# Two more PSUM evacuations per batch on ScalarE in the late light batches of a routed attention block

## The reference

```
mod = silu(c) @ wmod                      # six rows of 128 per batch: sa, ca, ga, sb, cb, gb
h = layernorm(x) * (1 + ca) + sa
x = x + ga * causal_attention(h)          # one head of 128, "attention"
h = layernorm(x) * (1 + cb) + sb
light  = local_attention(rmsnorm(h))      # 8 heads of 64, windows of 128 rows, then @ wo_light
scores = coordinate_descent(h . token)    # 50 iterations per batch and token, then top_k (128 of 256)
heavy  = attention(rows of h picked by the q scores, all rows weighted by the kv scores)
x = x + gb * (light + scatter(heavy))
```

## Time and profile before

| what | value |
|---|---|
| median of 3 runs | 482.2 us (480.55 to 482.89) |
| profiled execution, its own time | 482.58 us |
| its span | 480.7 us |
| PE busy | 445.8 us (93%) |
| DVE busy | 328.1 us (68%) |
| ACT busy | 345.6 us (72%) |
| POOL busy | 267.3 us (56%) |
| mean granted PE clock | 0.986 |

### The profile page before, as it was taken

One profiled execution on the slowest core, in us unless ns is written; L12 is line 12 of the kernel. 1 busy time (PEld: TensorE's weight loads), 2 busy tenths in 40 slices (PEclk: granted clock), 3 DMA queues, 4 the chain that ended last, 5 costly groups with the idle time before them and its releaser, 6 DMA issues.

```text
span 480.7 us, 12054 instructions
## 1 busy us (share of the span) xinstructions
PE 445.8 (93%) x4088; PEld 393.3 (82%) x4088; DVE 328.1 (68%) x1099; ACT 345.6 (72%) x1260; POOL 267.3 (56%) x325
## 2 busy tenths in 40 slices
PE   7858889999999999899997799999999999999994
PEld 6747688998989988787786688888888888888873
DVE  5874788778768897989879964555555454555551
ACT  3665989889788877677775678667776766677761
POOL 3147576576576776332332335544666666556555
PEclk9996999999999999999999999999999999999998
DMA  6880000001001001000000000100000010000002
GB/s 219 237 314 22 14 13 13 13 1 33 25 1 35 23 20 49 3 12 13 12 12 13 6 8 24 35 18 7 12 11 13 12 18 14 16 12 13 7 8 22
DMA packets 20108, 16.28 MB, mean 34 GB/s; under 512 B 1968, under 2 KB 18880, under 8 KB 19792
## 3 DMA queue, kind: packets, MB, share of 16 engines
q1 hardware_dynamic: 16480, 13.01, 8.8%
q0 software_dynamic: 2816, 2.10, 3.3%
q10 hardware_dynamic: 752, 0.40, 0.3%
HBM read 10.23 MB, written 5.28 MB: 32 GB/s over the span
## 4 chain that ended last, share of the span: by engine, by line
PE 64%; DVE 14%; ACT 5%; issue 4%; POOL 4%; POOLq 0%; ACTq 0%; DVEq 0%
PE bank L905 6%; PE bank L916 6%; PE bank L660 6%; PE bank L931 6%; PE bank L662 5%; PE bank L661 5%; PE bank L813 4%; PE bank L854 4%; PE bank L843 4%; PE bank L827 4%; ACT pr L591 3%; PE bank L872 3%; DVE cd_min L1208 3%; PE bank L944 3%; DVE nmx L1162 2%
## 5 line engine op out<-in xcount | busy, mean ns | idle before, releaser
L420 POOL TENSOR_TENSOR pr<-pr,rinv 128x512 f32<-128x512 f32 x64 | 66.5, 1040 | 84.2 <-DVE rinv L1168 84.2
L432 POOL TENSOR_TENSOR pr<-pr,rinv 128x512 f32<-128x512 f32 x64 | 72.7, 1155 | 63.8 <-DVE rinv L1313 63.8
L591 ACT ACTIVATE pr<-bank,nmx 128x128 f32<-128x128 f32 x256 | 90.5, 377 | 20.8 <-DVE nmx L1162 20.7
L634 ACT ACTIVATE pr<-bank,nmx 128x256 f32<-128x256 f32 x128 | 59.3, 485 | 19.3 <-DVE nmx L1307 19.3
L1307 DVE TENSOR_REDUCE nmx<-bank 128x2 f32<-128x512 f32 x64 | 41.9, 681 | 33.4 <-PE bank L905 33.4
L644 ACT ACTIVATE pt<-bank 128x512 f32<-128x512 f32 x64 | 38.2, 596 | 27.0 <-PE bank L916 27.0
L591 ACT ACTIVATION_READ_ACCUMULATOR pr<-bank,nmx 128x1 f32 x256 | 55.5, 217 | 0.0
L1162 DVE TENSOR_REDUCE nmx<-bank 128x4 f32<-128x512 f32 x64 | 42.8, 672 | 8.5 <-PE bank L813 8.4
L827 PE MATMUL bank<-ident,pr 128*128 128x128 f32 x256 | 38.9, 275 | 7.4 <-POOL pr L420 6.8
L916 PE MATMUL bank<-ident,pr 128*128 128x128 f32 x256 | 38.8, 274 | 1.6 <-ACT pt L644 1.6
L827 PEld LDWEIGHTS bank<-ident,pr 128*128 128x128 f32 x256 | 29.6, 141 | 10.6 <-POOL pr L420 8.5
(11 more groups left out here) (218 smaller groups left out, 1315.8 us busy)
## 6 DMA issues: line engine op xcount, KB each, us to landing
mod_bc<-mod_rows_scratch SPq DMA_DIRECT2D x1, 2560.0 KB, 15.4
X<-in_L_attn_x SPq DMA_DIRECT2D x4, 512.0 KB, 8.0
xh_scratch<-xhs SPq DMA_DIRECT2D x16, 128.0 KB, 1.9
out<-X SPq DMA_DIRECT2D x16, 128.0 KB, 1.8
mod_bc<-mod_rows_scratch SPq DMA_DIRECT2D x1, 1024.0 KB, 7.8
wkv_raw<-in_L_ffn_wkv_light SPq DMA_DIRECT2D x1, 512.0 KB, 7.6
mod_bc<-mod_rows_scratch SPq DMA_DIRECT2D x1, 512.0 KB, 3.8
wmod_sb<-in_L_wmod ACTq DMA_DIRECT2D x1, 384.0 KB, 5.3
```

The lines of the kernel that those rows point to most:

```text
L420: pool.tensor_tensor(q, q, rinv[u][:, :, None].broadcast_to([P, 4, P]), ALU.mult)\
L432: pool.tensor_tensor(q, q, rinv[u][:, 0:2, None].broadcast_to([P, 2, N]), ALU.mult)\
L591: act.activation(pr[u][:, i * P:(i + 1) * P], ps[bank][:, i * P:(i + 1) * P], ACT.Exp, bias=nmx[u][:, i:i + 1], accum_out=sums[u][:, i:i + ...
L634: act.activation(pr[u][:, i * N:(i + 1) * N], ps[bank][:, i * N:(i + 1) * N], ACT.Exp, bias=nmx[u][:, i:i + 1], accum_out=sums[u][:, i:i + ...
```

## The change

In batches 8 to 15 (those with 4b >= ACT_PT) two copies go from DVE to ACT: the values of window 1 (bank 7), right behind those of window 0 in ACT's `v_evac_l`, and the attention output of window 1 (bank 4), in a new entry `o_evac_late` at the head of ACT's list, in the same slot in which DVE had it. The semaphores and what they count stay the same. Batches 0 to 7 are as before.

```diff
                 act.activation(V[b % 2][:, 0, :], ps[0][:, :], ACT.Copy).then_inc(lt["va"], 1)
+                if 4 * b >= ACT_PT:
+                    act.wait_ge(lt["vp"], 2 * b + 2)
+                    at_least(act, lt["Op"], 2 * (b - 2) + 2)
+                    act.activation(V[b % 2][:, 1, :], ps[7][:, :], ACT.Copy).then_inc(lt["vd"], 1)
...
+            def o_evac_late(b):
+                if 4 * b >= ACT_PT:
+                    act.wait_ge(lt["Op"], 2 * b + 2)
+                    at_least(act, lt["outp"], b)
+                    act.activation(oT[1][:, :, :], ps[VALUE_BANKS[1]][:, :].rearrange("p (q t) -> p q t", q=4), ACT.Copy)\
+                        .then_inc(lt["oTd"], 1)
...
-            run_slots([("H", 8, pt_evac_h, 3), ("T", 0, cd_act), ("L", 5, v_evac_l), ("H", 3, k_evac_h),
+            run_slots([("L", 9, o_evac_late), ("H", 8, pt_evac_h, 3), ("T", 0, cd_act), ("L", 5, v_evac_l), ("H", 3, k_evac_h),
...
             def v_evac_l(b):
+                if 4 * b >= ACT_PT:
+                    return
                 dve.wait_ge(lt["vp"], 2 * b + 2)
...
             def o_evac_l(b):
+                if 4 * b >= ACT_PT:
+                    return
                 dve.wait_ge(lt["Op"], 2 * b + 2)
```

## The result

The changed kernel took 485.42 us (median of 9 runs, 484.50 to 486.69); the kernel before, 482.89 us (9 runs beside it). The ratio on record is 1.0069, with a 95% interval of 1.0049 to 1.0089: slower by 3.3 us of 482.9, between 2.4 and 4.3. The forecast was +4.0 us and 486.2.

What follows compares the result with a forecast made beforehand. PE was taken as the bound, delayed by ACT's late unit 2: light batches +2.65 us plus first heavy batch +1.35 gave +4.0 on 482.58, 486.6; the median, 0.4 lower, 486.2 us (8 in 10: 482.4 to 488.4).

Steps and rivals of the forecast that it cites:

- What bounds the kernel: PE bounds the heavy phase, so its shift through light batches 8 to 15 and the first heavy batch stays.
- ACT's packed piece: ACT's gapless copies and exponentials after unit 1, batches 8 to 15: unit 2's exponentials start 1.17 us later.
- A: Start of V's copy on ACT before the change; the output copy was to start there after it.
- The other signs: Profile after: DVE about 90% in 252 to 276 us, idle before unit 2's reciprocals; first heavy scores 2 to 3 us later.
- Rival A: DVE's time counts: 11 copies beside the selection gain 6.7 us less 1.35, so -5.3, 476.9 us; chance 0.09.
- C: Rival: all 1.17 us reaches PE in 8 batches, nothing earned in 11 and 12: +10.7, 493 us; chance 0.06.
- B: Rival: ACT's delay in batches 8, 9, 10, 14 (2.8 us) is swallowed before PE: +1.2, 483.4 us; chance 0.24.
- The terms: Batches 8 to 15: +0.6, +1.1, +0.6, -0.7, -0.5, +0.1, +0.5, +0.95 us; first heavy batch +1.35.
- Batch 10: Light batch 10: unit 1's transposes and the key projection come 0.6 us late, so +0.6 us.
- The heavy term: First heavy batch: batch 15's output copy delays heavy unit 1's exponentials on ACT by 1.6 us; PE loses 1.35 us.

Runs made afterwards that it cites:

- the value copies alone: Against the kernel before, only the value copies of window 1 in batches 8 to 15 go to ACT; 483.99 us, ratio 1.0025.
- the added row maxima: Changed kernel plus an unused 128x512 row maximum on DVE for each of 16 copies taken from it; 486.60 us, ratio 1.0091; again 486.18 us.

## Why the prediction was right

**What bounds the kernel.** Right: PE's delays in batches 8 to 15 and the first heavy batch stay to the end. Behind them 168.3 to 168.6 us follow in every profile. The nine periods give +3.9 us and the two comparisons of whole executions +3.3 and +2.7 us (0.57% of 482.4).

**ACT's packed piece.** Right, and shown by the value copies alone: in batch 14, exponentials of unit 2 at A + 1.66, their reciprocal 3.2 us behind A (forecast 3.13). The other signs came too: DVE at 92% in the stretch, idle in front of the reciprocals of batches 12 and 13, and the first heavy scores 2.4 us later than before, counted from batch 8's scores (301.59 - 186.93 against 300.71 - 188.46). The rule of the Trainium skill (Perfetto Trace Analysis, "Identifying the Most-Contended Engine") names DVE in this stretch, and DVE was the busiest; its relief in all batches was worth 1.2 to 1.6 us, and ACT's place took more. Rival A is out, and so is C. What B needs was not seen: batches 8, 9, 10 and 14, whose 2.8 us it takes to be swallowed, lost 2.5.

**The terms.** Eight of nine within 0.16 us. That the sum came within 0.1 us is partly luck: batches 10 and 11 came out 0.4 us below their terms together, and the others 0.35 us above theirs. That 485.42 lies near 486.2 owes something to the base as well, which read 482.2 then and 482.89 beside the changed kernel. The steps by which the delay reaches PE were followed in the traces for batches 10 and 14 and the heavy batch; for the others the periods fit the forecast, and the steps themselves are not shown.

Batch 10 was mis-sized: +0.6 forecast, +0.32 measured. I had carried the delay of the key projection as if its own gap stayed. PE's timeline from its start to unit 2's transposes behind it, before and after:

```profile
225.56 0.37 PE L660 MATMUL bank<-XT_hi,K_w_lo 128*128 128x256 f32 x1
...
226.25 0.28 PE L662 MATMUL bank<-XT_hi,K_w_hi 128*128 128x256 f32 x1
226.58 0.39 PE L660 MATMUL bank<-XT_hi,K_w_lo 128*128 128x256 f32 x1
...
227.39 0.60 PE L827 MATMUL bank<-ident,pr 128*128 128x128 f32 x4
```
```profile
226.33 0.39 PE L671 MATMUL bank<-XT_hi,K_w_lo 128*128 128x256 f32 x1
...
227.14 0.29 PE L671 MATMUL bank<-XT_hi,K_w_lo 128*128 128x256 f32 x1
...
227.86 0.60 PE L838 MATMUL bank<-ident,pr 128*128 128x128 f32 x4
```

Counted from the batch's scores, the projection starts 0.6 us later, as forecast (226.33 - 216.57 against 225.56 - 216.40). It took 1.83 us before, with a gap in the middle (226.25 to 226.58, where neighbours stand 0.12 apart), and 1.53 after, without one: the delay ate the gap.

The heavy term came out at +1.51 for +1.35. DVE's V copies start 1.51 us later, counted from the heavy scores (308.07 - 301.59 against 305.68 - 300.71), where the prediction has 1.47, and the query projection that waits for them starts 0.90 us behind their start both before (306.58) and after (308.97). The 0.1 to 0.2 us of slack that the prediction gave PE there was not there.

**What is left of the difference to the times.** The periods say +3.9, the runs +3.3 (2.4 to 4.3) and +2.7 (1.8 to 3.7). The interval of the first holds 3.9, that of the second ends just short of it. The clock accounts for some of it, which is an estimate: over all profiles taken, it fell ahead of batch 9 in 5 of 8 where PE's pause was 1.88 to 1.89 us, and in 2 of 6 where it was 1.69 to 1.70, both of them with the added row maxima; ahead of batch 13 in 2 of 8 at 1.70 to 1.71, and in none of 6 at 1.39 to 1.58. The kernel before has the pauses of 1.89 and 1.71 us and loses 0.84 or 0.82 each time: 5/8 x 0.84 + 2/8 x 0.82 = 0.7 us on average. The changed one has 1.70 and 1.40. It loses 2/6 x 0.44 = 0.15 if the row maxima had no part in those two falls, and nothing by its own two profiles, where the clock stayed up. That makes 3.9 - 0.6 = 3.3, or 3.2. With so few profiles the shares are rough (the kernel before by itself: 1 fall of 3 in either batch), and that the length of the pause decides is not shown: no run changed it alone.

## What to carry to other kernels

An engine's busy share over a stretch doesn't say where in the period its idle time lies; put work there, and look at what stands behind it in the same stream and at the latest of its inputs: here a wait of 0.2 us for PE and two copies moved 1.2 us of everything behind. When a software pipeline is moved by a rule for all batches, read its prologue and epilogue apart: the last instance of one copy met another neighbour and cost 1.5 us by itself. And choose by batch: the same two copies gained 0.8 us where DVE was late, and lost 1.1 us where the next step already waited for ACT.

## What the hardware showed that I had not expected

Between executions of the same kernel, PE's granted clock fell to 0.50 for about 3 us behind a pause of 1.7 to 1.9 us in some and stayed at 1.00 in others; a fall cost 0.4 to 0.8 us. None of the pauses of 1.39 to 1.59 us ahead of the scores of batches 13 and 14, 16 in the 14 profiles, was followed by one. But four pauses of 1.71 to 1.72 us ahead of batch 14's weren't either, so the length alone is not shown to decide. The part ahead of batch 8, the same in all kernels, ended between 186.3 and 188.7 us, and that spread is larger than most effects looked for here.
